# Tiles of 64 tokens of two batches in place of 128 tokens of one, in an mLSTM and fp4 feed-forward kernel

## What is computed

```python
qh, kh, vh = ...                      # 8 heads of 64; q = layernorm(x), k = v = ctx
ig, fg = gate_in @ igate_w.T + igate_b, gate_in @ fgate_w.T + fgate_b
log_f_cum = cumsum(log_sigmoid(fg))
log_D = where(tril, log_f_cum[s] - log_f_cum[t] + ig[t], -inf)
D = exp(log_D - max_log_D)
C = (qh @ kh.T / sqrt(dh)) * D
normalizer = maximum(abs(sum(C)), exp(-max_log_D))
h = (C / (normalizer + 1e-6)) @ vh    # then a norm per head, times norm_w
x = x + h
```

```python
h = silu(fp4_linear(x, w_gate)) * fp4_linear(x, w_up)      # 512 -> 1408
x = x + fp4_linear(h, w_down)                              # 1408 -> 512
```

## Time and profile before

| | |
|---|---|
| median of 3 runs | 1754.5 us (1754.49 to 1754.88) |
| profiled execution | 1753.9 us, span 1752.2 us |
| busy, of the span | PE 1679.3 (96%), DVE 1637.0 (93%), ACT 1297.4 (74%), POOL 1154.9 (66%) |
| mean granted TensorE clock | 0.984 |
| chain that ended last | PE 88% of the span |
| DMA engines | mean 137 GB/s, 574454 packets, 507520 of them under 512 B |

### The profile page before, as it was taken

One profiled execution on the slowest core, in us unless ns is written; L12 is line 12 of the kernel. 1 busy time (PEld: TensorE's weight loads), 2 busy tenths in 40 slices (PEclk: granted clock), 3 DMA queues, 4 the chain that ended last, 5 costly groups with the idle time before them and its releaser, 6 DMA issues.

```text
span 1752.2 us, 41405 instructions
## 1 busy us (share of the span) xinstructions
PE 1679.3 (96%) x13633; PEld 898.6 (51%) x13633; DVE 1637.0 (93%) x3455; ACT 1297.4 (74%) x2696; POOL 1154.9 (66%) x1188
## 2 busy tenths in 40 slices
PE   4568999999999999999999999999999999999998
PEld 3434555555555555555555555555555555555544
DVE  8998999999999989999998999999899999999996
ACT  7777777777777777787777778777777877767652
POOL 8876767567666766766666666666666666757663
PEclk9689999999999999999999999999999999999999
DMA  6446656566566656656665675665567566654423
GB/s 213 138 95 140 143 140 150 132 149 151 130 153 139 148 133 147 157 132 147 142 143 134 146 160 130 148 144 142 132 149 157 131 147 144 138 113 101 111 68 71
DMA packets 574454, 240.60 MB, mean 137 GB/s; under 512 B 507520, under 2 KB 514176, under 8 KB 574240
## 3 DMA queue, kind: packets, MB, share of 16 engines
q1 hardware_dynamic: 574240, 237.96, 58.4%
HBM read 140.35 MB, written 31.72 MB: 98 GB/s over the span
## 4 chain that ended last, share of the span: by engine, by line
PE 88%; DMA 0%; DVE 0%; ACT 0%; issue 0%; DVEq 0%
PE bank L523 50%; PE bank L654 9%; PE bank L656 8%; PE bank L655 8%; PE bank L622 4%; PE bank L539 4%; PE bank L616 2%; PE bank L634 2%; PE bank L584 1%; PE bank L594 0%; DMA xqT<-xqs 0%; DMA work<-stage 0%; PE bank L501 0%; DVE stage L1312 0%; DVE stage L1336 0%; DVE ob L1294 0%
## 5 line engine op out<-in xcount | busy, mean ns | idle before, releaser
L523 PE MATMUL bank<-wgTh,xqT 128*128 128x512 f16 (+1 forms) x1536 | 556.3, 362 | 7.5 <-DMA xqT<-xqs 6.4
L523 PE MATMUL bank<-wuTh,xqT 128*128 128x512 f16 (+1 forms) x1536 | 555.3, 362 | 0.0
L1102 POOL TENSOR_TENSOR stage<-stage,hs 128x512 f32<-128x512 f32 (+1 forms) x192 | 214.8, 1119 | 140.2 <-DVE stage L1317 138.5
L523 PE MATMUL bank<-wgTl,xqT 128*128 128x512 f16 (+1 forms) x768 | 277.8, 362 | 0.0
L523 PE MATMUL bank<-wuTl,xqT 128*128 128x512 f16 (+1 forms) x768 | 277.8, 362 | 0.0
L654 PE MATMUL bank<-wdTh,work 128*128 128x512 f16 x704 | 267.7, 380 | 3.3 <-DMA work<-stage 3.3
L655 PE MATMUL bank<-wdTl,work 128*128 128x512 f16 x704 | 267.1, 379 | 0.0
L656 PE MATMUL bank<-wdTh,work 128*128 128x512 f16 x704 | 267.0, 379 | 0.0
L523 PEld LDWEIGHTS bank<-wgTh,xqT 128*128 128x128 f16 x1536 | 150.2, 98 | 169.0 <-issue 10.9
L523 PEld LDWEIGHTS bank<-wuTh,xqT 128*128 128x128 f16 x1536 | 150.5, 98 | 147.4 <-issue 0.5
L1157 POOL TENSOR_TENSOR stage<-stage,hinv 128x512 f32<-128x512 f32 (+1 forms) x192 | 212.6, 1119 | 14.1 <-DVE hinv L1416 7.4
(11 more groups left out here) (210 smaller groups left out, 3656.5 us busy)
## 6 DMA issues: line engine op xcount, KB each, us to landing
mb<-max_dram SPq DMA_DIRECT2D x64, 512.0 KB
x<-in_x_dram SPq DMA_DIRECT2D x64, 256.0 KB, 2.9
wb<-warp_dram SPq DMA_DIRECT2D x128, 128.0 KB, 3.1
cn<-in_ctx_dram SPq DMA_DIRECT2D x64, 256.0 KB, 3.1
out_dram<-ob SPq DMA_DIRECT2D x64, 256.0 KB, 2.4
xb<-in_x_dram SPq DMA_DIRECT2D x60, 256.0 KB, 2.8
xh_dram<-xb SPq DMA_DIRECT2D x55, 256.0 KB, 2.3
xzb<-xh_dram SPq DMA_DIRECT2D x220, 64.0 KB, 2.5
```

What stands on the lines that cost most here:

```text
L523: i = e.matmul(o[:, 0:width], x, w[:, c, n0:n0 + width], start=first and k < 2, stop=last and k >= 4)
L1102: e.tensor_tensor(blocks(hx[:, n0:n0 + w]), blocks(hx[:, n0:n0 + w]), per_block(hs2[:, n0 // BLOCK:(n0 + w) // BLOCK]), ALU.mult).then_inc ...
```

## The change

A tile becomes 64 tokens of each of two batches, batch pair `p` (`first % 4`) and `chunk` (`first // 4`), so there are again 64 tiles, but four pairs of states and chunks of 64. Scores between the two batches aren't computed. With the keys of batch b in array rows of the head's parity and the results in the column half `par ^ b`, scores, both parts of u and the state sum are all products of 64x64 weights in the four quarters of the array. D has 128 x 512 entries in place of 128 x 1024; the exponentials are 64 columns each, the products with the scores 256. The running gate rows are 64 partitions of 64 columns, which makes the pick products eight and the turning of the rows eight small products with parts of `ident`.

The state is first scaled in place by GpSimd (`pool_St_old`), once u has read it, then VectorE adds the new sum in two additions. The new sum of the second batch lies in a gate bank of the feed-forward block, free once `silu[1]` of t8 has read it. Transfers of x and ctx come in two halves; for chunks from 3 (x) and from 2 (ctx) on, ScalarE's queue copies the chunk into `x_tiles` and `c_tiles` in DRAM beforehand (`act_stage_x`, `act_stage_c`, at the start of a turn with `u % 4 == 1`). The load of ScalarE's exponential table after `h_hi 0` is kept in every fourth turn only.

```diff
     def tokens(...)
-        return slice(t.first // 8 * P + t.slot * S, t.first // 8 * P + t.slot * S + P)
+        return dram[2 * t.p + b, t.chunk * S2:(t.chunk + 1) * S2, :]
...
         def pe_qk(e, t):
...
             for c in range(HC):
-                for par in range(2):
-                    r = slice(par * DH, (par + 1) * DH)
-                    i = e.matmul((R0, R1)[par][:, c * P:(c + 1) * P], cT[r, t.slot, c, :], xT[r, t.slot, c, :], start=True, stop=True)
+                for b in range(2):
+                    for par in range(2):
+                        r = slice(par * DH, (par + 1) * DH)
+                        i = e.matmul((R0, R1)[par][HALF[par ^ b], c * S2:(c + 1) * S2], cT[r, t.slot, c, HALF[b]], xT[r, t.slot, c, HALF[b]],
+                                     start=True, stop=True)
...
         def pe_u(e, t):
...
+            def old(c, b):
+                for par in range(2):
+                    r = HALF[par]
+                    i = e.matmul(U[par][HALF[b], c, :], xw[r, b, c, :], St[t.p][r, b, c, :], start=(c == 0), stop=False)
+            def new(c, b):
+                for k in range(2):
+                    r, par = HALF[k], k ^ b
+                    i = e.matmul(U[par][HALF[b], c, :], D[r, par, c, :], vc[t.parity][r, 2 * c + par, :], start=False, stop=(c == HC - 1))
+            old(0, 1)
+            for c in range(1, HC):
+                i = old(c, 1)
+                old(c - 1, 0)
+            i.then_inc(S_["u_old"], 1)
+            e.wait_ge(S_["vc"], t.done())
+            e.wait_ge(s_C[1], t.done())
+            old(HC - 1, 0)
+            new(0, 0)
+            new(1, 0)
+            e.wait_ge(S_["u_old"], t.done())
+            new(0, 1)
+            for c in range(2, HC):
+                new(c, 0)
+                new(c - 1, 1)
+            new(HC - 1, 1).then_inc(S_["u"], 1)
...
         def pe_st_mm(e, t):
+            elif t.has(4):
+                e.wait_ge(s_silu[1], t.done(2))
             for c in range(HC):
                 for par in range(2):
-                    i = e.matmul(R1[par * DH:(par + 1) * DH, c * DA:(c + 1) * DA],
-                                 cn[:, h * DH:(h + 1) * DH], vk[:, h, :], start=True, stop=True)
+                    for b in range(2):
+                        h, r = 2 * c + par, HALF[par ^ b]
+                        i = e.matmul(state_sum(t, b)[HALF[par], c, :], cn[r, h * DH:(h + 1) * DH], vk[r, h, :], start=True, stop=True)
...
+        def act_stage_c(e, g):
+            if g > 2:
+                e.wait_ge(S_["c_tiles"], 48 * (g - 2))
+            src = ctx_in[:, at, :].rearrange("(p b) s e -> b p s e", b=2)
+            for k in range(3):
+                e.dma_start(c_tiles[4 * g:4 * g + 4, k * S2:(k + 1) * S2, :], src[k % 2]).then_inc(S_["c_tiles"], 16)
...
-            e.preload_act_table_set(EXP_LN)
+            if t1.live(NT) and t1.slot % 4 == 3:
+                e.preload_act_table_set(EXP_LN)
...
+        def pool_St_old(e, t):
+            e.wait_ge(S_["wb_in"], t.of(64, 63))
+            e.wait_ge(S_["u"], t.done())
+            last = wb[:, :, :, S2 - 1].unsqueeze(3).broadcast_to([P, 2, HC, DA])
+            e.tensor_tensor(St[t.p][:, :, :, :], St[t.p][:, :, :, :], last, ALU.mult).then_inc(S_["St_old"], 1)
...
         def dve_St(e, t):
-            for c in range(HC):
-                i = e.scalar_tensor_tensor(St[t.slot][:, c, :], St[t.slot][:, c, :], wb[:, c, P - 1:P], ST[:, c, :], ALU.mult, ALU.add)
+            for b in range(2):
+                i = e.tensor_tensor(St[t.p][:, b, :, :], state_sum(t, b), St[t.p][:, b, :, :], ALU.add)
```

More of the change, by code:

```diff
@@ L35 @@
     parity = property(lambda self: self.first % 2)
+    p = property(lambda self: self.first % 4)
+    chunk = property(lambda self: self.first // 4)
     def live(self, total):
@@ L338, in sp_x_in @@
                 e.wait_ge(S_["xh_out"], 16 * (t.first - 9))
-            e.dma_start(xb[:, :], x_rows[tokens(t), :]).then_inc(S_["x_in"], 16)
+            if x_staged(t):
+                e.wait_ge(S_["x_tiles"], 32 * (t.chunk - 2))
+                e.dma_start(xb[:, :], x_tiles[t.first]).then_inc(S_["x_in"], 16)
+                return
+            for b in range(2):
+                e.dma_start(xb[b * S2:(b + 1) * S2, :], tokens(x, t, b)).then_inc(S_["x_in"], 16)
         def sp_xh_out(e, t):
@@ L510, in pe_gu @@
                 e.wait_ge(s_xqT[t.parity], t.dma(2))
+                if t.has(3) and t.back(-1).live(NT):
+                    e.wait_ge(S_["St"], t.done(-1))
+            if t.at_start(0) and n == 1:
+                e.wait_ge(S_["St"], T[1].done())
             if n == 2:
@@ L1244, in pool_turn @@
                 pool_vk(e, t6)
+                pool_St_old(e, t6)
             if t7.live(NT):
@@ L1453, in dve_a @@
                     e.wait_ge(S_["row_T"], t.quads(4))
-                e.tensor_tensor(rows[0:QR, :], ig[:, :], F[:, :], ALU.add).then_inc(S_["gate"], 1)
+                e.tensor_tensor(rows[0:GR, 0, :], ig[:, :], F[:, :], ALU.add).then_inc(S_["gate"], 1)
         def dve_M(e, t):
```

310 lines of the change are left out of this document (184 added, 126 removed).

## The result

The changed kernel takes **2227.98 us** (median of 4 runs, 2221.93 to 2230.32) beside 1754.49 for the kernel before on the same chip: ratio 1.2696, 95% interval 1.2667 to 1.2724. The forecast of 1734 and its range of 1720 to 1800 are both wrong, and so is the direction. By ratio each version is compared with runs of the kernel before on its own chip; differences between versions are differences of medians.

The account below looks back on a forecast made before the run. The prediction took TensorE to bound the kernel, with VectorE next. Its terms, -48 + 16 + 3 + 6 + 2 = -21 us, gave a median of 1734 us against 1754.5, with a range of 1720 to 1800 (chance 0.80).

Parts of the forecast that it names:

- What bounds the kernel before: Whole kernel: TensorE, busy all of 101.96 us in four turns, sets the time; VectorE is next at 96.24.
- TensorE, plain turn: Scores 1.09 to 0.65 us, three phases 2.18 to 1.82: 0.80 less a turn, minus 48 us over 60 turns.
- that rival: TensorE's scores and values: quarters don't overlap, plus 45 us, with gate turns 1815 us; chance 0.05.
- TensorE, gate turn: Pick products plus 0.7 us (1.1 in all), turning the rows plus 0.4; fifteen such turns, plus 16 us.
- GpSimd's St_old ahead of x_qs, +3: GpSimd's state scaling delays x_qs, leaving xqT 0.6 us slack where 2.0 was: 0.05 us a turn, plus 3 us.
- VectorE, "Cost: nothing": VectorE needs 0.6 us less a turn; spare time goes from 1.4 to 1.2 and covers the 0.96 hold: no cost.
- ScalarE's five copies, +6, 15 groups: Issuing five copies takes ScalarE 2.6 us once in four turns: 0.4 us a chunk, 15 chunks, plus 6 us.
- SyncE, "Nothing": SP's queue: five more transfers a turn, 2.7 us, issuing 15 us of 25; near 4 us to spare, no cost.
- Start, +2: Start: twelve more small picks, 2.9 us, ahead of GpSimd's first scaling, partly hidden in waiting: plus 2 us.
- staged copies block the queue's transfers: The five DRAM copies: 64 KB runs delay transfers behind them, 3.6 to 4.5 us a chunk, 1794 us; chance 0.27.
- The signs named beforehand: Wrong if TensorE waits over 0.5 us in copy turns, silu holds VectorE over 1 us, or picks exceed 1.5 us.

Follow-up runs that it names:

- e9: e1 with GpSimd's two masks exchanged, so that the one over 128 partitions runs directly ahead of the burst: 1902.74 us.
- e11: The changed kernel without the copies (loads read 128 successive tokens of the inputs) and with GpSimd's two masks swapped: 1826.94 us.
- e12: The changed kernel with copies in 2 KB runs on sixteen engines, one or two a turn over four turns, and GpSimd's masks swapped: 1864.62 us.
- e16: e12 with x_qs ahead of the scaling of the state St_old on GpSimd: 1860.79 us.
- e5: The changed kernel without the copies, its loads reading 128 successive tokens straight from the inputs: 1961.51 us.
- e1: The changed kernel with the token as the copies' slowest dimension, so 2 KB runs on sixteen engines in place of 64 KB on four: 2008.21 us.
- e13: e12 with SyncE's row reordered: xh out directly behind xqT, then cn and wb, the load of xb, then cf: 1863.07 us.
- e18: e17 with SyncE's row in the order of e13: 1840.06 us, ratio 1.0488.
- e17: e16 with tile 2's state sum and tile 3's scores moved ahead of tile 1's products in TensorE's row of the start: 1856.45 us.
- e4: The kernel before with the five copies a chunk alone added, into DRAM tensors that nothing reads: 2086.84 us, ratio 1.1878.
- e7: e1 with VectorE's xs, xt and xi moved to where GpSimd's burst of five multiplications is over: 1912.47 us.

## Why the prediction was wrong, point by point

**What bounds the kernel before:** right. It was TensorE, and the copies and the mask, put into it alone, each turned that over.

**TensorE, plain turn:** right. The starts of the phases in the changed kernel (products with the state, first down product, scores, next gate and up product):

```profile
1081.45 0.74 PE L689 MATMUL bank<-St,xw 64*64 64x65 f32 x32
...
1083.29 0.39 PE L748 MATMUL bank<-wdTh,work 128*128 128x512 f16 x1
...
1090.51 0.69 PE L609 MATMUL bank<-xT,cT 64*64 64x64 f32 x32
1091.14 0.39 PE L592 MATMUL bank<-wgTh,xqT 128*128 128x512 f16 x1
```

The three phases take 1.84 us (1.82 was said, give 2.18), the scores 0.63 (0.65; 1.09). Where nothing waits the turn takes 24.05 us in e9, e11 and e12, and 24.86 - 0.80 is 24.06. Quarters overlap; that rival is out.

**TensorE, gate turn:** right in kind, too small. The pick products, against the earlier trace rows, and the product that follows them:

```profile
1241.16 1.61 PE L667 MATMUL bank<-gpart,pick 128*128 128x64 f32 x16
```

```profile
1242.70 0.34 PE L592 MATMUL bank<-wgTh,xqT 128*128 128x384 f16 x1
```

1.54 us in place of 0.43 where 1.1 was said. Turning the rows takes 0.57 (1250.26 to 1250.83 us) in place of 0.11 (955.72 to 955.83); the prediction took the 0.27 of one product's length for what it takes of the row. The gate turn of e11 is 28.25, that is 4.20 over the plain one, 2.52 before: plus 1.7 and not 1.1, 25 us in all and not 16. With -48 this would still be a gain of 23.

**GpSimd's St_old ahead of x_qs, +3:** not refuted. Taking that order away gave 4 us at most (e16), and TensorE's wait for xqT didn't go with it. But e16 didn't bear out my second theory either, that these 3 us had been 50: St_old's waits for u went from 29.0 us to 3.8 between 1000 and 1340 us, TensorE's for xqT rose from 12.3 to 18.9.

**VectorE, "Cost: nothing":** wrong, and worth 135 us (e5 to e11), the second of the large errors. The step that failed is "Cost: nothing": it listed what gets shorter on VectorE and never looked at what GpSimd can hold up there. The new kernel's `pool_mask` shows a mask over `S2 * (k + 1)` partitions, and the earlier trace rows say nothing of it: I had priced GpSimd's own added time alone. No row of the kernel before shows an instruction on 64 partitions ahead of that burst, so at least a bound was due: VectorE's xs can be held for the burst, 5 us a turn against the 1.2 of spare time that the step itself left.

**ScalarE's five copies, +6, 15 groups:** wrong, and the largest error. The term counts the time to issue the copies, 2.6 us of ScalarE's row, and puts at nothing what their transfers do to all others. Measured are 266 us (e5 to the changed kernel). The first chunks are copied in the start, and the third tile's products come 33 us later there (233.4 against 200.8); the other 233 us are 19 for each of the twelve groups that stand in turns, where 0.4 was said. On sixteen engines five copies in one turn cost 47 us (e5 to e1), spread ones 38 (e11 to e12).

**SyncE, "Nothing":** wrong with the copies, where wb's four issues stood 22.7 us. Without them ScalarE waits for xb 22 us in eight turns; the order that shortens this wait is worth 2 us alone (e13) and 16 beside other edits (e18).

**Start, +2:** wrong. Without copies the third tile's products start 30 us later than before (199.8 against 169.6). In e11 8 us of them stand ahead of the first tile's gate and up products (118.3 against 110.3) and 21 between the first and the second (49.0 against 28.2). The order of TensorE's row there moves the third tile by 7.7 (205.75 in e16, 198.04 in e17) and the median by 4. What makes the other 22 us stays open.

**The rival *staged copies block the queue's transfers*:** the right mechanism, with a chance of 0.27 and a price four to five times too low: 60 us where the copies cost 266 in the changed kernel and 333 alone. The step of it that failed is "Price: 3.6 to 4.5 us of TensorE per chunk". It took the length of one run for what a transfer waits; a transfer can wait for all that the copies have queued on the engine it needs, ten runs, 10 x 2.48 = 24.8 us (xqT landed 28.8 us after its issue in e4; wb's first pieces in the changed kernel after 12 and 14). And it priced only the landings, where SyncE's issues stand still as well. The sentence beside it had the number: by the Trainium skill's rule on how many engines a transfer gets ("DMA: Bandwidth & Descriptors", section "Why a DMA increments its semaphore by 16 and not by 1") it gave four engines and 36 us of them per chunk. The trace agrees on the four engines, with 24.9 us. Worked on to an end it would have said: SyncE needs a transfer several times in every turn, so a chunk loses 36 us less a few, 12 x 30 = 360. The rival's "against", that the copies are only 2.6 MB in 100 us, is an average over sixteen engines of what four of them carry. Its other half, that the next transpose is some 9 us off, was wrong: xqT is issued at 1119.86 us and the copies from 1120.32 on.

**The signs named beforehand.** Two came: TensorE waits 5.6 us for xqT in the turn of the copies, where 0.5 was the limit, and the pick phase takes 1.54 us, where 1.5 was. The third, silu holding VectorE by over 1 us, came too (5.8 us at the longest between 1000 and 1200 us), there behind TensorE's own waits.

**The sum.** In medians, taken away in this order: copies 2228 - 1962 = 266, the mask ahead of the burst 1962 - 1827 = 135, and the rest of the change 1827 - 1754 = 73, of which 30 lie in the start, 39 in the steady stretch and 3 behind it (e11's trace). The parts don't simply add: put alone into the kernel before, the copies cost 333 and the mask 156. The change's own gain on TensorE, 23 to 32 us, is there but is never seen: in e11 two turns of four stand above 24.05 us, by 1.8 and 1.4.

## What to carry to other kernels

Count for a transfer how many DMA engines its outermost dimension gives it, and price the bytes per engine, not the bytes: a queue that is busy 4% on average can hold up another one's transfers and issues for 24 us. When an instruction on GpSimd gets another number of partitions, look at which VectorE instructions run beside what follows it, and keep full-width instructions directly ahead of a burst. An instruction that is busy twenty times as long as the same one elsewhere is a wait, and no view of waits shows it.

## What the runs showed of the hardware that I had not expected

- GpSimd, one instruction over 64 of 128 partitions ahead of five multiplications back to back: a 128x32 TENSOR_SCALAR on VectorE takes 4.96 to 4.99 us, until the last of them ends; over 128 partitions 0.93 to 0.96, until the first ends; with GpSimd idle 0.23. Two other forms are held as well: 128x512 `dve_h_q` for 3.97 and `dve_h_lo` for 3.22 (0.68 otherwise, e7). A product read from PSUM (128x256, 0.41) and a 128x512 TENSOR_REDUCE (0.67) beside the same burst aren't.
- 512 KB DRAM to DRAM with an outermost dimension of 4 goes through four engines at 2.48 us for 64 KB each. With 64 outermost and 2 KB runs the kernel takes 2008.2 us, with 16 and 8 KB runs 2006.7.
- While four engines are taken, issues can stand: 22.7 us for four on SyncE, and up to 4.6 us for each of the copies' own on ScalarE where the runs are 1 KB.
